# Cross attention on one core: score products on 56 rows for both passes, value products in one group per turn

## The reference, cut to what matters

```python
q = einsum('oc,bct->bot', Wq, target) + bq      # k and v likewise, from source
q, k, v -> (b, 16 heads, 16 channels, 512 positions)
dot = einsum('bhdt,bhds->bhts', q, k) / math.sqrt(16)
mask = target_mask[..., :, None] * source_mask[..., None, :]
dot = mask * dot - (1.0 - mask) * 1e6
amap = softmax(dot, axis=-1) * mask
out = einsum('bhts,bhds->bhdt', amap, v)
```

## Time and profile before

| what | value |
|---|---|
| median of 3 runs | 2806.84 us (2806.16 to 2814.8) |
| the profiled execution | 2802.59 us, span 2801.0 us |
| cross attention's loop over the sequences | from 1444.1 to about 2318 us of the span |
| PE busy, of the span | 2603.9 us (93%) |
| DVE busy | 1875.0 us (67%) |
| ACT busy | 1455.1 us (52%) |
| POOL busy | 995.5 us (36%) |
| mean granted clock of PE | 0.97 |

### The profile page before, as it was taken

The page is one execution under the profiler, slowest core; times in us unless marked ns, Lnnn a source line. Parts: engine busy times, 40 slices in busy tenths (PEclk is TensorE's granted clock), DMA queues, the critical chain, the costliest instruction groups (busy, mean ns, idle before and its releaser), DMA issues. The chain is left out here.

```text
span 2801.0 us, 51111 instructions
## 1 busy us (share of the span) xinstructions
PE 2603.9 (93%) x15536; PEld 1816.8 (65%) x15537; DVE 1875.0 (67%) x3845; ACT 1455.1 (52%) x2868; POOL 995.5 (36%) x1178
## 2 busy tenths in 40 slices
PE   7999999999999999999759999999999986399997
PEld 6888888888888888888524444444443423277775
DVE  6556655566544455554569898889888876576665
ACT  4334433345433344333337777777777765255554
POOL 1112211112111112211235665665665647433332
PEclk9999999999999999999879999999999988699999
DMA  4102222013201111111154555555655558655554
GB/s 150 69 7 75 75 75 75 26 49 136 91 31 61 45 45 60 60 47 43 53 123 118 133 136 136 139 131 136 139 135 130 133 147 287 230 101 106 111 106 83
DMA packets 140817, 282.49 MB, mean 101 GB/s; under 512 B 39344, under 2 KB 42288, under 8 KB 135616
## 3 DMA queue, kind: packets, MB, share of 16 engines
q1 hardware_dynamic: 112416, 214.99, 26.7%
q0 software_dynamic: 23664, 58.09, 10.0%
q10 hardware_dynamic: 4656, 8.40, 1.0%
HBM read 147.82 MB, written 81.68 MB: 82 GB/s over the span
## 5 line engine op out<-in xcount | busy, mean ns | idle before, releaser
L1566 DVE TENSOR_REDUCE b_negmax<-b_ps_s 128x2 f32<-128x1024 f32 x512 | 611.2, 1218 | 52.9 <-PE b_ps_s L1751 46.4
L278 POOL TENSOR_SCALAR probs<-probs,rinv 128x256 f32<-128x256 f32 x256 | 242.0, 945 | 1094.3 <-DVE rinv L435 1094.3
L1366 ACT ACTIVATE b_probs<-b_ps_s 128x1024 f32<-128x1024 f32 x512 | 520.0, 1020 | 198.9 <-PE b_ps_s L1762 197.6
L312 ACT ACTIVATE probs<-ps_s,negmax 128x128 f32<-128x128 f32 x256 | 94.1, 367 | 484.5 <-DVE negmax L428 484.5
L1775 PE MATMUL b_ps_o<-b_probs,b_v_stack 128*32 128x256 f32 (+1 forms) x2816 | 295.0, 491 | 0.9 <-ACT b_probs L1366 0.8
L1762 PEld LDWEIGHTS b_ps_s<-b_stack 56*128 56x128 f32 x1024 | 96.3, 184 | 272.4 <-issue 165.7
L1762 PE MATMUL b_ps_s<-b_stack 56*128 56x512 f32 x1024 | 257.6, 500 | 15.4 <-DVE b_negmax L1566 7.5
L1751 PE MATMUL b_ps_s<-b_stack 54*128 54x512 f32 x1024 | 228.7, 443 | 42.4 <-DMA b_stack<-b_split 24.0
L543 PE MATMUL ps_proj<-xT_h,wq_h 128*128 128x512 f32 x512 | 216.0, 422 | 0.0
L2461 POOL DMA_INDIRECT out<-e_y,e_place_int x71 | 118.1, 1664 | 253.4 <-DMA out<-e_y,e_place_int 218.4
L543 PE MATMUL ps_proj<-xT_h,wq_l 128*128 128x512 f32 x512 | 201.7, 394 | 0.0
(11 more groups left out here) (334 smaller groups left out, 6641.1 us busy)
## 6 DMA issues: line engine op xcount, KB each, us to landing
b_stack<-b_split SPq DMA_DIRECT2D x336, 128.0 KB
e_row<-rows_by_expert SPq DMA_DIRECT2D x71, 258.0 KB, 2.9
b_out_tiles<-row_sum_inverses SPq DMA_DIRECT2D x64, 256.0 KB
x<-acc SPq DMA_DIRECT2D x15, 1024.0 KB, 4.8
x_in<-in_x SPq DMA_DIRECT2D x8, 1024.0 KB, 8.1
normalised_x_split<-xT_h SPq DMA_DIRECT2D x8, 1024.0 KB, 9.8
normalised_x_split<-xT_l SPq DMA_DIRECT2D x8, 1024.0 KB, 11.0
acc<-in_x SPq DMA_DIRECT2D x8, 1024.0 KB, 11.3
```

The costliest lines, as they stand in the source:

```text
L278: nc.gpsimd.tensor_scalar(probs[:, s, P:3 * P], probs[:, s, P:3 * P], rinv[:, s, 1:2], None, ALU.mult).then_inc(probs_done, 1)
L312: nc.scalar.activation(probs[:, s, 0:P], ps_s[s][:, 0:P], ACT.Exp, bias=negmax[:, s, 0:1], accum_out=rowsum[:, s, 0:1])
L1366: nc.scalar.activation(probs[:, k % 2, p, :, :], ps[:], ACT.Exp, scale=0.25).then_inc(e_done, 1)
L1566: nc.vector.tensor_reduce(negmax[:, k, p, :], ps[:], AX.X, ALU.max, negate=True).then_inc(m_reduced, 1)
```

## The change

The key side of the last two rows stays 1, the query side now starts at 0, so that a product over 56 rows adds 0 to the scores of the maximum pass. The maximum pass uses the 56 rows. The products with the values are one group in all turns, after M0; the second half after M1 is gone.

```diff
-                aux_op(nc.vector.memset(max_rows, 1.0))
+                nc.vector.memset(max_rows[:, :, 0, :], 0.0)
+                aux_op(nc.vector.memset(max_rows[:, :, 1, :], 1.0))
...
                     for i in range(2):
-                        rows = slice(SIDE * i, SIDE * i + MAXROWS)
+                        rows = slice(SIDE * i, SIDE * i + EXPROWS)
                         ins = nc.tensor.matmul(ps[:, i, :], stack[rows, quad, 0, p, k * P:(k + 1) * P],
                                                stack[rows, quad, 1, p, :], start=True, stop=True)
...
-                def values_product(g, q, k, part=0, parts=1):
-
-                    cols = slice(T // parts * part, T // parts * (part + 1))
-                    if part == 0:
-                        pe.wait_ge(e_done, UNITS * g + 2 * k + 2)
-                        if k == 0:
-                            pe.wait_ge(v_done, g + 1)
-                            pe.wait_ge(o_out, g)
+                def values_product(g, q, k):
+
+                    pe.wait_ge(e_done, UNITS * g + 2 * k + 2)
+                    if k == 0:
+                        pe.wait_ge(v_done, g + 1)
+                        pe.wait_ge(o_out, g)
                     for h in range(HQ):
-                        ins = nc.tensor.matmul(ps_o[32 * h:32 * h + 32, cols], v_stack[:, k, HQ * q + h, :],
-                                               probs[:, k % 2, h // 2, h % 2, cols], start=(k == 0 and part == 0), stop=(k == TBL - 1))
-                    if k == TBL - 1 and part == parts - 1:
+                        ins = nc.tensor.matmul(ps_o[32 * h:32 * h + 32, :], v_stack[:, k, HQ * q + h, :],
+                                               probs[:, k % 2, h // 2, h % 2, :], start=(k == 0), stop=(k == TBL - 1))
+                    if k == TBL - 1:
                         ins.then_inc(o_filled, 1)
...
-                        parts = 2 if k > 0 and (q, k) not in PIECES else 1
...
-                                    values_product(g + q, q, k - 1, 0, parts)
+                                    values_product(g + q, q, k - 1)
...
-                        if parts == 2:
-                            values_product(g + q, q, k - 1, 1, parts)
```

## The result

The changed kernel takes 2823.93 us (median of 4 runs, 2820.89 to 2827.73), the kernel before 2807.14 in the same job (4 runs): a ratio of 1.0057, 95% interval 1.0041 to 1.0073, or 16.8 us slower. The profiled executions are 2821.72 (span 2818.8) and 2802.59 (span 2801.0): +19.1 us. The forecast was +19, the profiled execution at 2822 and the median at 2826.

A forecast was written before the change was run, and what follows sets the result against it. PE and DVE were taken as near each other, neither able to run ahead with three PSUM buffers, M0 waiting for ACT's exponential. Terms of 1.32 us a sequence gave 20.0, taken as +19: 2826 us median (profiled 2822), range 2803 to 2838.

The forecast's parts named there:

- 56 rows at 0: Maximum pass on 56 rows instead of 54: claimed to change nothing, 0 us, with ends of 7 us either way.
- The memsets at 0: Two memsets for one, before the first score products: claimed 0 us, 0.1 us if uncovered; ends 0 and +1.8.
- Quad 1, +0.75: Turns (1,1) to (2,0): M0 waits 1.62 us after E1 for ACT, so E0 of (2,0) comes about 0.75 us later a sequence.
- Turn (2,3), +0.42: Turn (2,3) into (3,0): E0 to E1 grows from 1.24 to 1.66 us and all behind moves with it, +0.42 a sequence.
- Turns (3,1), (3,2), +0.15: Quad 3 to the next sequence's (0,1): the chain moves with ACT's exponential of (3,3), +0.16, taken as +0.15 us a sequence.
- PE's 0.55 is nearly all inside the 0.52: At the next sequence's E0 of (0,1): its 0.52 us wait for DVE covers nearly all of PE's 0.55 us delay.
- The sum: Whole loop: 0.75 + 0.42 + 0.15 = 1.32 us a sequence, less in sequences 14 and 15, 20.0 us in all.
- The deduction from 20.0 to 19: Whole loop: in some sequences a late load already makes PE or DVE wait and takes up a part, so +19 us.
- The signs named: Changed kernel's trace: 2048 value matmuls, M nearer 0.5, turns of 3.04 us, sequence of 54.6, E0 of (0,1) waiting for DVE.
- B: Rival: quad 1's delays meet waits in quad 2, the rest slack at (0,1); +5 us, 2812, or less; chance 0.14.
- C: Rival: nothing absorbed, PE's 0.55 in quad 3 counts whole; 1.72 us a sequence, +26, 2833; chance 0.74 together with the forecast.
- A: Rival: in the six merged turns PE was the bound and switches are won; -23 us, 2784; chance 0.12.

## Why the prediction was right

**56 rows at 0:** right, within what can be measured. The rows show a gain of 0.15 us a sequence that the interval can't confirm.

**The memsets at 0:** two of 912 ns in place of one of 1765, 1.82 us in all (0.06 more, of the 0.1 allowed for a start), and the loop's first E is not later (1443.55, before 1444.11).

**Quad 1, +0.75:** measured +0.76, and +0.77 alone. The step that carried it, 1.62 from E1 to the M0 that takes its buffer, was read from one turn of the old kernel and holds in all turns without a piece. That (1,1) hides its 0.42 is shown by the two kernels that merge only there and in (3,2): that stretch gets shorter.

**Turn (2,3), +0.42:** measured +0.42, and +0.4 alone.

**Turns (3,1), (3,2), +0.15:** mis-sized; measured +0.35, and +0.4 alone. PE and ACT reach the seam late as worked out: (3,1) to (3,3) grow by 0.61 in all, (3,3) by 0.80 of it. What failed is the step "PE's 0.55 is nearly all inside the 0.52". The start of sequence 9 in the kernel after:

```profile
1938.14 0.50 PE L1763 MATMUL b_ps_s<-b_stack 56*128 56x512 f32 x2
1938.35 0.60 ACT L1372 ACTIVATE b_o_sb<-b_ps_o 128x512 f32<-128x512 f32 x1 [0.31 <-PE b_ps_o L1774]
1938.85 1.02 ACT L1366 ACTIVATE b_probs<-b_ps_s 128x1024 f32<-128x1024 f32 x1
1939.37 0.50 PE L1763 MATMUL b_ps_s<-b_stack 56*128 56x512 f32 x2
1939.92 0.50 PE L1752 MATMUL b_ps_s<-b_stack 56*128 56x512 f32 x2
1940.35 1.07 PE L1774 MATMUL b_ps_o<-b_probs,b_v_stack 128*32 128x512 f32 x8
```

And the two fills of the kernel before that compare with 1938.14 and 1939.92:

```profile
1924.57 0.50 PE L1762 MATMUL b_ps_s<-b_stack 56*128 56x512 f32 x2
...
1926.69 0.40 PE L1751 MATMUL b_ps_s<-b_stack 54*128 54x512 f32 x2
```

E0 of (0,1) at 1939.37 no longer waits for DVE, as it did for 0.52 in the earlier trace rows. But M0 needs the buffer of the E at 1938.14, whose exponential starts only at 1938.85, behind the copy of the context, and ends at 1939.87. So M0 comes 1.78 after that E; before, with the wait, it came 2.12 after. The wait of 0.52 could give back only 0.34, since the next one stood right behind it. V then comes 0.43 behind an M that waited, 0.10 more than behind one that ran through.

**The sum.** Sequences 0 to 12 cost 20.15 us more (694.32 to 714.47) where the terms gave 13 x 1.32 = 17.2. Sequences 13 to 15 as a stretch cost nothing (178.1 and 178.2), where the forecast had 2.8 for them. Late transfers take it up. In (2,0) of sequences 13 and 14 the kernel before waits 0.76 and 0.66 us for rows of the stack, and the turn takes 3.90 and 3.77; after, it takes 2.86 and 2.85. At the end of sequence 14 and the start of 15, PE waits for a late transfer of the rows of maxima and then for DVE, in the kernel before 3.07 and 2.91 us, after it

```profile
2266.95 0.50 PE L1763 MATMUL b_ps_s<-b_stack 56*128 56x512 f32 x2 [1.21 <-DMA b_stack<-b_nm_rows]
...
2271.65 0.80 PE L1752 MATMUL b_ps_s<-b_stack 56*128 56x512 f32 x2 [4.20 <-DVE b_negmax L1567]
```

The first wait swallows 1.9 us of delay, the second gives 1.3 back. And one turn in the router's work, (3,1) of sequence 15, takes 9.68 for 10.53, which no edit touches. The deduction from 20.0 to 19 was right in kind, but too small for these three sequences, while the terms were too small for the others: two errors of 2 to 3 us cancelled. The +19.1 of the profiled execution is made up of 20.21 from the loop's first E to its last, less 0.56 ahead of it, less 1.85 behind it, where no edit touches anything (484.44 before, 482.59 after; it was 481.0 to 487.7 us over the kernels run), and 1.33 around the span. So the mechanism was right, and that the profiled execution met 2822 to the microsecond is luck. The median moved by 16.8, and the ratio's interval makes that 11.5 to 20.5.

**The signs named.** Met: 2048 value matmuls of 512, the idle time before M from ACT, 3.04 in (1,2), (1,3) and (3,2), the busy time of DVE and ACT. The sequence of 54.8 lies 0.2 over the 54.6 and between the marks of B (53.8) and C (55). Missed: the mean duration of M, 429 ns against 431, did not go to 500; and E0 of (0,1) does not wait for DVE.

**The rivals.** A needed E1 to M0 below 1.2; it is 1.62. Its saving is real on PE: M1 to E0 with no layout change between is 0.24 (1904.80 to 1905.04), against 0.33 to 0.34 next to one, and PE's busy time went down by 1.3 us a sequence. PE spends it waiting, and more (2.4 us a sequence before M). By the Trainium skill, TensorEngine Tiling (Array Packing), "Key Properties", a change of tiling mode drains TensorE; the trace agrees that it costs, about 0.1 us on the side of the score pair (though 1901.88 to 1902.21 is 0.33 with no change between, so the price is not cleanly read). But that rule alone gave the wrong sign, since a buffer and not the array decided. B needed the delays of quad 1 to meet slack in quad 2; (2,0) to (2,2) changed by 0.10 in all. C, a whole 0.55 at the seam, overrates it: 0.35 to 0.4 came.

## What to carry to other kernels

With a ring of three PSUM buffers, the time from a fill to the fill that reuses its buffer has a floor: start of the reader, the reader's duration, release (here 0.54 + 1.02 + 0.06 = 1.62 us). Filler work should be split so that each such interval has some of it; here one lump of 0.99 us stood beside the hold instead of inside it, and what the merging saved on the engine, 1.3 us a sequence, was spent in waiting. And where a delay is to be hidden in a wait, read what comes due just behind that wait: 0.34 of 0.52 us was all that was to be had.

## What the runs showed that was not expected

- An exponential of 128x256 from PSUM takes 380 ns, one of 128x1024 1020: a quarter of the elements for 0.37 of the time.
- Freeing ACT made this kernel slower: the turns of quad 1 together became 1.3 us shorter, but DVE waited up to 3.05 us for a transfer of row sums that nobody had waited long for, PE stood for 2 us behind it, and then PE's granted clock fell from 1.00 to 0.50 for a few microseconds. The stand and the clock cost more than was gained.
- Two DVE instructions of 0.24 and 0.30 us, moved by one turn, made two turns of PE 0.6 us longer each (3.68 for 3.08, 3.50 for 2.91): in the first PE waits for DVE, in the second for a transfer into the stack.
